# Waiting for each gather's landing by itself, with at most four gathers in flight, in a graph kernel's edge stage

## The chip, the cores and the metric

The kernel is one program on one core of a Trainium2 chip. The metric is the device time of one execution in microseconds (us), as the median of several runs.

## The reference

A layer on 3125 nodes of 256 features and 50,000 edges, sorted by destination. It adds to x a graph attention layer (8 heads, softmax over each destination's edges), a linear attention layer, and then a mixture of 16 experts, two for each node. What the change touches is the first:

```
def _L0_gnn_ref(x, edge_index, W, att_src, att_dst, ...):
    h = jnp.einsum('nf,hfd->hnd', x, W)
    a_s = jnp.einsum('hnd,hd->hn', h, att_src)
    a_d = jnp.einsum('hnd,hd->hn', h, att_dst)
    e = jax.nn.leaky_relu(a_s[:, src] + a_d[:, dst], 0.2)
    def head_step(acc, xs):
        h_h, e_h, g_h = xs
        m = jax.ops.segment_max(e_h, dst, num_segments=N)
        ex = jnp.exp(e_h - m[dst])
        den = jax.ops.segment_sum(ex, dst, num_segments=N)
        alpha = ex / den[dst]
        out = jax.ops.segment_sum(h_h[src] * alpha[:, None], dst, num_segments=N)
        return (acc + g_h * out, None)
...
xn = _layernorm(x, axis=-1)
x = x + gnn(xn, edges) + mix(xn)
x = x + ffn(_layernorm(x, axis=-1))
```

## The kernel before

Stages follow one another: projections and tables for the edges (up to about 190 us), the edge stage (190 to 1000 us), the output of both attentions, the experts, and the last sum. The edge stage holds the change.

The sum over edges is done on the features before W is applied, weighted for 8 heads. The 50,000 edges lie in 391 chunks (`CHUNKS`) of 128 edges. Destinations lie in 196 windows of 16 nodes. A step is a pair (chunk, window) that share an edge: the two lists are merged, so there are 391 + 196 - 1 = 586 steps, padded to 592, in 37 groups of `G` = 16. A chunk whose edges span two windows serves in two steps. Early windows have many edges, late ones few, so early groups take more new chunks than late ones.

For each chunk GpSimd gathers 128 rows of `node_rows` (272 floats each: 256 normalised features, a one, 8 source scores, padding; 128 x 1088 B = 136 KiB) into one slot of the ring `rows`, which has `RING` = 48 slots. The indices are a column of `srcT`. Nothing else runs on GpSimd in this stage, apart from five gathers of `gad` (64 KB each) at its start.

Readers of a slot are ScalarE's `copy_as` (L830, copies the source scores of 16 chunks to `asb`) and TensorE's `product` (L947, a matmul of `pw` with the chunk's row block into one of five PSUM banks `pO`). The order of a turn of the group loop is written out by hand for each engine in `groups([...])`. With tau as the turn, `copy_as` works at group tau, the scores, the running maxima and the exponentials at group tau - 1, the products, VectorE's `accumulate` (L790) and SyncE's stores of `agg_rows` (L986, two of 1 MB a group, 8 steps each) at group tau - 2. `accumulate` is a recurrence: each step's `acc` is the step's before, times `rsc` (L757 and L761, from TensorE's L922), plus the product.

Before `copy_as` of a group reads, ScalarE loads 16 slot numbers and the number of chunks needed into registers, then waits:

```
upto_chunk = act.value_load(step_tab[0:1, g, G:G + 1], min_val=1, max_val=CHUNKS)
act.wait_ge(fetched, upto_chunk)
```

GpSimd's queue before works in fours of gathers (`FETCH` = 4, 98 fours, the last of three). For a four that overwrites old slots, it loads a step number from `free_at` into a register (L679) and waits until so many products are done (`prod`, L680, a gate, with an increment of `s_gate` behind it at L681). The value belongs to the last of the four chunks being overwritten. It then issues four gathers that all raise the same one of two semaphores `s_rows`, and after that waits until the four before have landed and adds four to `fetched` (`landed`, the wait and the increment being one instruction, L675). At the time of that wait up to eight gathers may be under way.

The start of the stage also needs loads that SyncE issues: `adsd`, the bias `bg`, `WoT`, `bob`. VectorE waits for the last of them before its first work.

Of the kernel before, what the change touches and what calls it, by code (L numbers as in the profile page):

```python
# [29 lines left out]
CHUNKS = -(-NE // P)  # L30
# [3 lines left out]
G, HG = 16, 8  # L34
GROUPS = -(-STEPS // G)
# [5 lines left out]
RING, FETCH = 48, 4  # L41
FETCHES = -(-CHUNKS // FETCH)
# [84 lines left out]
def at_row(ap):  # L127
    return bass.IndirectOffsetOnAxis(ap=ap, axis=0)
# [32 lines left out]
def build(nc, a, out):  # L161

    with ExitStack() as top:
        def dram(name, shape, dt=F32):
            return nc.dram_tensor(name, shape, dt, kind="Internal").ap()

        def sb(name, shape, dt=F32, ctx=top):
            return ctx.enter_context(nc.sbuf_tensor(name, shape, dt))
# [4 lines left out]
        def sem(name):  # L173
            return top.enter_context(nc.semaphore(name))

        node_rows = dram("node_rows", (NP, RW))
# [44 lines left out]
        srcT = sb("srcT", [P, CHUNKS], U32, edge_ctx)  # L221
        step_tab = sb("step_tab", [1, SP_ // G, TAB], I32, edge_ctx)
        free_at = sb("free_at", [1, FETCHES], I32, edge_ctx)
# [365 lines left out]
        with ExitStack() as ctx:  # L589
# [5 lines left out]
            rows = sb("rows", [P, RING, RW], ctx=ctx)  # L595
# [39 lines left out]
            betaR = sb("betaR", [P, KD, P], ctx=ctx)  # L635
            v_cw, cw_ps = sem("v_cw"), sem("cw_ps")
            consts.expect(5)
            s_rows = [sem(f"s_rows{c}") for c in range(2)]
            s_flg, s_top = [sem(f"s_flg{c}") for c in range(V2)], sem("s_top")
            s_agg = [sem(f"s_agg{c}") for c in range(V3)]  # L640
            fetched, as_in = sem("fetched"), Count(sem("as_in"))
# [24 lines left out]
            with nc.Block() as block:  # L666
                @block.gpsimd
                def _(pool):

                    for j in range(SJ):  # L670
                        pool.indirect_dma_start(gad[:, j, :], None, ad_rows.rearrange("(w d) h -> w (d h)", d=DW), at_row(rowc[:, 1, j:j + 1])).then_inc(s_gad, 16)

                    def landed(q):
                        pool.wait_ge(s_rows[q % len(s_rows)], 16 * FETCH * (q // len(s_rows)) + 16 * len(range(q * FETCH, min((q + 1) * FETCH, CHUNKS))))
                        pool.sem_inc(fetched, len(range(q * FETCH, min((q + 1) * FETCH, CHUNKS))))  # L675

                    for q in range(FETCHES):
                        if q * FETCH >= RING:
                            steps = pool.value_load(free_at[0:1, q:q + 1], min_val=1, max_val=GROUPS * G)  # L679
                            pool.wait_ge(prod.sem, steps)  # L680
                            pool.sem_inc(s_gate, 1)  # L681
                        for k in range(q * FETCH, min((q + 1) * FETCH, CHUNKS)):
                            pool.indirect_dma_start(rows[:, k % RING, :], None, node_rows[:, :], at_row(srcT[:, k:k + 1])).then_inc(s_rows[q % len(s_rows)], 16)  # L683
                        if q:
                            landed(q - 1)
                    landed(FETCHES - 1)

                @block.vector
                def _(dve):
# [1203 lines left out]
```

## Time and profile before

| | us |
|---|---|
| median of 3 runs (lowest, highest) | 1812.19 (1808.88, 1820.98) |
| the profiled execution | 1812.91 |
| its span on the core | 1810.8 |
| TensorE busy in the span (matmul) | 1220.3 (67%) |
| VectorE | 1053.7 (58%) |
| ScalarE | 486.0 (27%) |
| GpSimd | 673.9 (37%) |
| mean DMA rate | 138 GB/s |

The span is the time from the first to the last instruction that the profile has. Busy time leaves out register, branch and semaphore instructions, so that a share says how long an engine computed, and not how near it is to being the limit. The ends of matmuls are modelled.

### The profile page before, as it was taken

What the parts mean: (1) busy time and instruction counts of PE and PEld (TensorE: products, weight loads), DVE (VectorE), ACT (ScalarE), POOL (GpSimd) and SP (SyncE); (2) the same over time, 40 slices, a digit from 0 to 9 for tenths busy, and PEclk for the clock granted to TensorE, in tenths of its full rate; (3) what the DMA queues carried; (4) which work ended last, traced back from release to release, by engine and by line L of the source; (5) the groups of instructions that cost most, each with busy time, mean ns of one, the idle gap of its engine ahead of it and who ended that gap; (6) DMA issues with size and microseconds to landing.
All of it is one profiled execution on the core that took longest, in us unless ns stands there. A gap on an engine that the chain in (4) does not pass through costs nothing. (4 is left out here: it accounts for less than half of the span.)

```text
span 1810.8 us, 29517 instructions
## 1 busy us (share of the span) xinstructions
PE 1220.3 (67%) x6148; PEld 994.7 (55%) x6149; DVE 1053.7 (58%) x3010; ACT 486.0 (27%) x1900; POOL 673.9 (37%) x781
## 2 busy tenths in 40 slices
PE   0795035666666776777784474999999179999800
PEld 0574023444444555555553353899998168999700
DVE  7656124556555666677785455678887433444357
ACT  0342011112221222222220233555553023333200
POOL 3000655656555454454300354244443201111164
PEclk9998556778887788897896656899999589999955
DMA  6015535566565656666644422334331395222155
GB/s 206 19 37 80 139 84 176 176 187 191 180 203 176 195 176 197 193 201 190 196 148 117 129 64 76 123 126 145 130 130 65 117 312 188 70 70 72 56 145 147
DMA packets 216712, 254.97 MB, mean 141 GB/s; under 512 B 53540, under 2 KB 190374, under 8 KB 212902
## 3 DMA queue, kind: packets, MB, share of 16 engines
q1 hardware_dynamic: 174262, 137.89, 24.9%
q0 software_dynamic: 30848, 103.40, 19.1%
q10 hardware_dynamic: 11504, 12.59, 2.1%
q8 instruction: 35, 0.57, 0.1%
q14 instruction: 63, 0.52, 0.1%
HBM read 138.88 MB, written 111.65 MB: 138 GB/s over the span
## 5 line engine op out<-in xcount | busy, mean ns | idle before, releaser
L683 POOL DMA_INDIRECT rows<-node_rows,srcT x391 | 381.7, 976 | 313.1 <-PE pO L947 179.7
L947 PE MATMUL pO<-rows,pw 128*128 x1184 | 381.1, 457 | 120.5 <-DVE pw L774 87.7
L790 DVE SCALAR_TENSOR_TENSOR acc<-acc,rsc,pO 128x257 f32<-128x257 f32 x592 | 282.4, 477 | 160.2 <-PE pO L947 74.0
L947 PEld LDWEIGHTS pO<-rows,pw 128*128 128x128 f32 x1184 | 243.0, 225 | 177.9 <-issue 143.2
L1355 PE MATMUL pW_<-W_again,aT 128*128 128x256 f32 x800 | 181.8, 381 | 0.0
L1355 PEld LDWEIGHTS pW_<-W_again,aT 128*128 128x128 f32 x800 | 148.9, 191 | 18.4
L1689 PEld LDWEIGHTS pHe<-xeT,w1e 128*128 128x128 f32 x1056 | 129.7, 194 | 9.9 <-DVE w1e L1727 6.6
L1689 PE MATMUL pHe<-xeT,w1e 128*128 128x128 f32 x1056 | 130.5, 277 | 5.7 <-DVE xeT L1707 4.8
L1745 POOL DMA_DIRECT2D ys_rows<-ye x66 | 35.7, 541 | 244.5 <-DVE ye L1737 244.5
L1698 PE MATMUL pYe<-w,hT 128*128 x528 | 125.3, 380 | 1.9 <-ACT hT L1668 1.1
L1668 ACT ACTIVATE hT<-pHe,b 128x128 f32<-128x128 f32 x264 | 75.5, 368 | 184.2 <-PE pHe L1689 172.7
L1698 PEld LDWEIGHTS pYe<-w,hT 128*128 128x128 f32 x528 | 95.2, 190 | 13.2 <-issue 3.0
L1406 DVE SCALAR_TENSOR_TENSOR own<-AG,al,own 128x256 f32<-128x256 f32 x200 | 94.8, 489 | 11.1 <-DMA AG<-agg_rows,lr 9.7
L830 ACT ACTIVATE asb<-rows 128x8 f32 x592 | 74.5, 209 | 70.0 <-issue 68.0
L774 DVE TENSOR_TENSOR pw<-pexp,eq 128x1024 f32<-128x1024 f32 x74 | 87.3, 1221 | 0.0
L1287 POOL DMA_INDIRECT xs_rows<-ysc,slot_x x50 | 49.4, 987 | 100.6 <-DVE slot_x L1510 91.7
L928 PE MATMUL pS<-topl,eq 128*128 128x72 f32 x148 | 29.4, 331 | 81.8 <-DVE topl L766 43.5
L1299 ACT ACTIVATE own<-xna,al 128x256 f32 (+1 forms) x200 | 82.2, 500 | 3.2 <-PEq L1039 2.5
L928 PEld LDWEIGHTS pS<-topl,eq 128*128 128x128 f32 x148 | 23.5, 227 | 96.2 <-DVE topl L766 53.9
L1727 DVE COPY w1e<-w 128x1024 f32 x66 | 45.8, 694 | 52.4 <-issue 39.0
L1707 DVE COPY xeT<-pXe 128x256 f32<-128x256 f32 x66 | 28.0, 424 | 79.6 <-PE pXe L1679 79.6
L1344 PE MATMUL pa<-cst,own 128*128 128x128 f32 x400 | 52.0, 286 | 18.6 <-DVE own L1406 18.6
(319 smaller groups left out, 2015.4 us busy)
## 6 DMA issues: line engine op xcount, KB each, us to landing
agg_rows<-acc SPq DMA_DIRECT2D x74, 1024.0 KB
w<-in_ffn_w SPq DMA_DIRECT2D x32, 512.0 KB, 5.6
xe<-xs_rows ACTq DMA_DIRECT2D x66, 128.0 KB, 2.0
ys_rows<-ye POOLq DMA_DIRECT2D x66, 128.0 KB, 2.0
rows<-node_rows,srcT POOLq DMA_INDIRECT x391
node_rows<-xna SPq DMA_DIRECT2D x25, 136.0 KB
xna<-in_x SPq DMA_DIRECT2D x5, 640.0 KB, 11.3
qs<-qT_y SPq DMA_DIRECT2D x25, 128.0 KB, 2.2
```

The costliest lines, as they stand in the source:

```text
L683: pool.indirect_dma_start(rows[:, k % RING, :], None, node_rows[:, :], at_row(srcT[:, k:k + 1])).then_inc(s_rows[q % len(s_rows)], 16)
L774: dve.tensor_tensor(pw[:, i, :, :].rearrange("p s (d h) -> p s d h", h=H), pexp[:, g % V2, s, :].unsqueeze(2).to_broadcast([P, HG, DW, H]) ...
L790: dve.scalar_tensor_tensor(out=acc[:, k % V3, s % HG, 0:D + 1], in0=before, scalar=rsc[:, g % V2, s:s + 1], in1=pO[n % PB][:, 0:D + 1], op ...
L830: ins = act.activation(asb[:, g % V2, s, :], rows[:, ds(at[s], 1), AS:AS + H].rearrange("p c h -> p (c h)"), ACT.Copy)
L928: mm = pe.matmul(td_ps[:, i * MW:(i + 1) * MW], eq[:, g % V3, i * HG:(i + 1) * HG, :].rearrange("p s d -> p (s d)"), topl[:, g % V2, i * H ...
L947: pe.matmul(pO[n % PB][:, 0:D + 1], pw[:, s // HG, s % HG, :], rows[:, ds(at[s % 4], 1), 0:D + 1].rearrange("p c f -> p (c f)"), start=Tru ...
L1299: ins = act.activation(own[:, c, h, :], tile(xna, t, 0, D), ACT.Copy, scale=al[:, 1, t, h:h + 1] if isinstance(t, int) else al[:, 1, ds(t, ...
L1355: mm = pe.matmul(pW[:, 0:D], aT[:, c, n, :], W[:, n % KD, n // KD, :], start=(n == 0), stop=(n == H * KD - 1))
L1406: ins = dve.scalar_tensor_tensor(out=own[:, c, h, :], in0=AG[:, c, h, :], scalar=al[:, 0, t, h:h + 1] if isinstance(t, int) else al[:, 0, ...
L1668: ins = act.activation(hT[:, c % 2, f, :], pH[c % 2][:, f * P:(f + 1) * P], ACT.Relu, bias=b1[:, ds(e, 1), f:f + 1].rearrange("p e f -> p ...
L1689: mm = pe.matmul(pH[c % 2][:, f * P:(f + 1) * P], w1e[:, c % S3, k, f * P:(f + 1) * P], xeT[:, c % 2, k, :], start=(k == 0), stop=(k == KD ...
L1698: mm = pe.matmul(pY[c % 2][:, 0:D], hT[:, c % 2, f, :], of_expert(w2, e, f), start=(f == 0), stop=(f == FK - 1))
```

## The change

GpSimd's queue goes gather by gather. There are four semaphores `s_rows`, and gather k raises number k mod 4. Before gather k is issued, gather k - 4 must have landed; that wait is one instruction with an increment of `fetched` by one. The gate is asked where it was asked before, at every fourth gather, behind that wait. The last four landings are waited for at the end. Ring, gate values, order of the gathers and all readers stay.

```diff
-            s_rows = [sem(f"s_rows{c}") for c in range(2)]
+            s_rows = [sem(f"s_rows{c}") for c in range(4)]
...
-                    def landed(q):
-                        pool.wait_ge(s_rows[q % len(s_rows)], 16 * FETCH * (q // len(s_rows)) + 16 * len(range(q * FETCH, min((q + 1) * FETCH, CHUNKS))))
-                        pool.sem_inc(fetched, len(range(q * FETCH, min((q + 1) * FETCH, CHUNKS))))
-
-                    for q in range(FETCHES):
-                        if q * FETCH >= RING:
-                            steps = pool.value_load(free_at[0:1, q:q + 1], min_val=1, max_val=GROUPS * G)
+                    def landed(k):
+                        pool.wait_ge(s_rows[k % len(s_rows)], 16 * (k // len(s_rows) + 1))
+                        pool.sem_inc(fetched, 1)
+
+                    for k in range(CHUNKS):
+                        if k >= len(s_rows):
+                            landed(k - len(s_rows))
+                        if k >= RING and k % FETCH == 0:
+                            steps = pool.value_load(free_at[0:1, k // FETCH:k // FETCH + 1], min_val=1, max_val=GROUPS * G)
                             pool.wait_ge(prod.sem, steps)
                             pool.sem_inc(s_gate, 1)
-                        for k in range(q * FETCH, min((q + 1) * FETCH, CHUNKS)):
-                            pool.indirect_dma_start(rows[:, k % RING, :], None, node_rows[:, :], at_row(srcT[:, k:k + 1])).then_inc(s_rows[q % len(s_rows)], 16)
-                        if q:
-                            landed(q - 1)
-                    landed(FETCHES - 1)
+                        pool.indirect_dma_start(rows[:, k % RING, :], None, node_rows[:, :], at_row(srcT[:, k:k + 1])).then_inc(s_rows[k % len(s_rows)], 16)
+                    for k in range(CHUNKS - len(s_rows), CHUNKS):
+                        landed(k)
```

## Rows read from the trace of the kernel before

A row of a timeline is: start us, duration us, engine, line, operation, names, count, and in brackets the idle time before it and its releaser. "issue" is idle time in which the engine waited for nothing that the profile shows; "remote" is a releaser that the profile matched to no instruction.

**Rows 1.** Groups of instructions by line, 192 to 970 us.
```profile
L683 POOL DMA_INDIRECT rows<-node_rows,srcT x391 | 381.7, 976 | 313.1 <-PE pO L947 179.7 <-issue 111.1 <-remote 21.8
L947 PE MATMUL pO<-rows,pw 128*128 x1180 | 380.3, 458 | 120.5 <-DVE pw L774 87.7 <-issue 31.5
L790 DVE SCALAR_TENSOR_TENSOR acc<-acc,rsc,pO 128x257 f32<-128x257 f32 x587 | 280.0, 477 | 159.7 <-PE pO L947 74.0 <-remote 38.7 <-issue 28.0
...
L830 ACT ACTIVATE asb<-rows 128x8 f32 x592 | 74.5, 209 | 70.0 <-issue 68.0 <-POOLq L675 1.6
```

**Rows 2.** Windows, accumulations of L790 alone: busy us (count), clock, DMA share, GB/s.
```profile
256.00:576.00 320.00, 108.62 (x228) 0.76 0.59 178
576.00:896.00 320.00, 133.11 (x280) 0.83 0.63 192
896.00:970.00 74.00, 38.23 (x81) 0.91 0.43 145
```

**Rows 3.** Windows, all engines (the count behind POOL is gathers).
```profile
256.00:576.00 320.00, 204.16 (x789) 149.17 (x790) 176.69 (x441) 64.18 (x384) 178.98 (x182) 0.76 0.59 178
576.00:896.00 320.00, 235.03 (x962) 172.66 (x963) 215.34 (x545) 75.84 (x446) 157.13 (x161) 0.83 0.63 192
```

**Rows 4.** Instructions of lines 675, 679, 681 on GpSimd's queue.
```profile
L675 POOLq EVENT_SEMAPHORE  x98: 17/17/17, 198.8 to 889.9; - x98
...
L679 POOLq TENSOR_LOAD <-free_at x86: 283/290/974, 249.2 to 876.6; - x86
L679 POOLq FUSED_REGOPS  x86: 147/147/186, 249.7 to 876.9; - x86
...
L681 POOLq EVENT_SEMAPHORE  x86: 17/17/17, 265.5 to 882.2; - x86
```

**Rows 5.** GpSimd's timeline, four of the gathers.
```profile
377.61 0.94 POOL L683 DMA_INDIRECT rows<-node_rows,srcT  x1 [5.07 <-issue]
...
405.86 0.95 POOL L683 DMA_INDIRECT rows<-node_rows,srcT  x1 [1.14 <-issue]
...
568.23 0.94 POOL L683 DMA_INDIRECT rows<-node_rows,srcT  x1 [2.62 <-issue]
...
783.01 0.94 POOL L683 DMA_INDIRECT rows<-node_rows,srcT  x1 [2.25 <-issue]
```

**Rows 6.** The tile rows, its gathers: duration ns, first and last start.
```profile
L683 POOL DMA_INDIRECT rows<-node_rows,srcT x391: 940/946/1961, 192.0 to 885.5; - x196
```

**Rows 7.** Timeline of all engines at two stretches.
```profile
233.01 0.45 PE L922 MATMUL pC<-shm,cst 128*128 128x16 f32 x2
...
243.37 0.28 ACT L858 ACTIVATE pexp<-pS 128x128 f32<-128x128 f32 x1 [11.25 <-remote]
...
251.32 0.95 POOL L683 DMA_INDIRECT rows<-node_rows,srcT  x1 [0.31 <-issue]
253.86 0.17 DVE L757 TENSOR_TENSOR rsc<-pC,firstT 128x16 f32<-128x16 f32 x1 [21.78 <-remote]
...
328.25 0.94 POOL L683 DMA_INDIRECT rows<-node_rows,srcT  x1 [0.30 <-issue]
...
331.56 0.48 DVE L790 SCALAR_TENSOR_TENSOR acc<-acc,rsc,pO 128x257 f32<-128x257 f32 x1 [7.76 <-remote]
```

**Rows 8.** The tile rsc: what ended VectorE's idle time before it (us, times).
```profile
  remote: 85.8, 21
```

**Rows 9.** Landings of the tiles gad, then agg_rows (its gathers).
```profile
DMA to landing us min/median/max: 2.4/2.6/2.8
...
DMA to landing us min/median/max: 5.5/5.8/7.9
```

**Rows 10.** Timeline at the stage's start.
```profile
212.83 0.56 DVE L697 TENSOR_SCALAR betaR<-cst,gam 128x128 f32<-128x128 f32 x2 [26.34 <-DMA bob<-in_bo]
...
221.81 1.37 ACT L830 ACTIVATE asb<-rows 128x8 f32 x11 [1.67 <-issue]
```

**Rows 11.** Window, all engines, 200 to 220 us.
```profile
200.00:220.00 20.00, 2.74 (x6) 1.47 (x6) 6.01 (x16) 0.24 (x1) 14.79 (x16) 0.50 0.85 208
```

## The prediction

> **What bounds the kernel now.** I began with the groups of instructions by line between 192 and 970 us, the edge stage, because the change touches nothing outside it [rows 1]. The reader is to see that no engine is full there: TensorE's products are 380 us of 778, VectorE's accumulation 280 us, and GpSimd's 391 gathers 382 us, with 313 us idle before them. 180 us of that idle time end with a TensorE product: it is the gate that frees slots of the ring.
>
> Then the windows [rows 2, 3]. Accumulations per window give the pace of the recurrence: 320/228 = 1.40 us a step from 256 to 576 us, 320/280 = 1.14 us from 576 to 896, and 74/81 = 0.91 us once the gathers are over (the last starts at 885.5 [rows 6]). GpSimd issued 182 and 161 gathers in the first two. At 0.91 us a step these 508 steps would take 464 us in place of 640. So 176 us of the stage go with the presence of gathers, though no engine shows that it waits for one.
>
> Where they go is seen in the timeline of all engines [rows 7]. TensorE's last matmul of the first group is recorded at 233.01 us; VectorE, which needs it, starts at 253.86 after 21.78 us idle, "remote", and ScalarE, which needs the one before, is late by 11.25 us. GpSimd issues 48 gathers in a row, the last at 251.32 for 0.95 us, so that VectorE goes on 1.6 us after it. At 331.56 the same: an accumulation has waited 7.76 us for a product recorded long before, and goes on 2.4 us after the run's last gather ended (328.25 + 0.94). I read this as TensorE's results being seen late while GpSimd issues back to back. There are 21 such waits of VectorE on this chain, 85.8 us in all [rows 8].
>
> **The change part by part.** *Signals.* The wait and the increment of `fetched` are one instruction of 17 ns on GpSimd's queue, 98 times before [rows 4]; there will be 391. The 293 more are 293 x 0.017 = 5.0 us of queue time, spread over a cadence of 1.25 us (0.95 busy, 0.30 issue) in which the queue already does 0.29 + 0.15 us of register work for every fourth gather [rows 4]. Cost 0; without that cover it would be 5 us.
>
> *When `fetched` rises.* Before, four arrivals are told at once, after the next four are issued; while the gate holds those back, the telling waits too. After, the first of four is told ahead of the gate and the other three behind it, each ahead of one more issue. So ScalarE hears earlier, by up to 5 us. Who waits for that? ScalarE's copies `asb` waited for this signal 1.6 us in all 37 groups, and 68.0 us for their own register loads ("issue") [rows 1]. TensorE reads the same chunks two groups later. Gain 0, at most 1.6 us.
>
> *The cap.* This is the wait that is added. Gather k now needs gather k-4 landed. Before, the first of a four needed the last of the four before the previous one, gather k-5, so a landing had 5 x 1.25 = 6.25 us, and now it has 4 x 1.25 = 5.00 us. Before, seven of the 97 boundaries between fours have a gap with releaser "issue" above the usual 0.30, the largest 1.14 us at 405.86 [rows 5]: landing plus reaction reached 6.25 + 0.84 = 7.1 us there, and stayed within 6.25 at the other 90. The trace gives these gathers no landing time. Nearest below are the gathers of `gad`, 64 KB each, 2.4 to 2.8 us; above, those of 1 MB from `agg_rows`, 5.5 to 7.9 us [rows 9]. One of these is 136 KB, nearer the small one. So most land well inside 5.0 us and are not delayed, and those beside a 1 MB store of `agg_rows` are. Each delay is between 0 and 7.1 - 5.0 = 2.1 us. On GpSimd that is at most 97 x 2.1 = 204 us of the 313 idle; I take 1 us beside each of the 64 stores of the groups that still have gathers, 64 us. Queued behind a blocked wait are only the next gathers and their signals, and for them ScalarE waits, once a group.
>
> What hides it is the ring's lead. ScalarE reads a group two groups ahead of the products. At 182/228 = 0.80 gathers a step, three groups of 16 steps hold 38 chunks of the ring's 48; 10 chunks, 12 steps x 1.40 = 17 us, are to spare. Later, at 161/280 = 0.58, it is 28 chunks, and 20 x 1.14 / 0.58 = 39 us are. A landing later by 2 us is not felt through `fetched`. Without the lead the 64 us would fall on the path.
>
> *Code.* Three gaps stand in the middle of a four, 5.07, 2.62 and 2.25 us, 112 gathers apart [rows 5]. I take them for GpSimd's instructions arriving late. The rows show 112 + 28 + 28 x 3 = 224 instructions for 112 gathers [rows 4]; after the change they are 112 + 112 + 28 x 3 = 308, so such a gap comes every 112 x 224/308 = 81 gathers: four in place of three, 2.3 to 5.1 us more of GpSimd's idle time, inside the 17 us. Cost 0.
>
> *The start.* VectorE waits 26.34 us for the load of `bob` until 212.83 [rows 10], while the gathers take their share of a DMA that is 0.85 busy at 208 GB/s [rows 11]. If the cap holds back up to three gathers of 139 kB there, the loads gain 0.42 MB / 208 GB/s = 2.0 us at most. I take 1. The 16 gathers that ScalarE needs at 221.81 are issued by 192.0 + 15 x 1.25 = 210.8; 11 us cover a slip.
>
> *Runs of gathers.* A gap for a landing lengthens a run. If results of TensorE come late until the run has ended, they come later by the gap: 21 waits x 0 to 2.1 us, 0 to 44 us. I take +2, near the lower end, since 90 of 97 boundaries kept within 6.25 us. That it frees something instead is the first rival.
>
> **The sum**: 1812.9 (the profiled execution; its span is 1810.8) - 1 + 2 = 1814. The median of the three runs is 0.7 lower than that execution, so 1813 us.
>
> **The rivals.** *Faster, because the cap eases TensorE.* What the 176 us go with is gathers in flight or back to back, and the cap thins them just where a store runs beside them. For it: the pace follows the number of gathers (182: 1.40, 161: 1.14, none: 0.91). Against it: the longest late result, 21.8 us, has an even cadence of 1.25 us beside no store, and if a landing takes 2.6 us there, two are in flight and the cap touches nothing. A quarter of 176 is 44 us, 1769; an eighth is 1791. It decides once a gap inside a run lets a pending result through.
>
> *Slower, because the runs end later.* 21 waits x 1 to 2.1 us = 21 to 44 us, 1834 to 1857. It decides from the point where landing plus reaction beside a store passes 5.0 us in nearly every group. For it: seven boundaries passed even 6.25. Against it: 90 did not.
>
> *The change does nothing*, because four are never in flight: 2.6/1.25 is two. Then 1812, within "same".
>
> *TensorE is not touched by gathers at all*, and the 176 us have another cause, such as fewer chunks a step. Then only the loads gain, 0 to 2 us: 1811 to 1813, within "same" too. The trace speaks against it, as late results and slow pace end with the gathers [rows 2, 7]; 0.1 of the 0.53 below is its. It is what the Trainium skill, "SBUF — State Buffer", section "SBUF: two separate sides", has: engine ports and DMA ports are disjoint, and TensorE waits for nobody there.
>
> **How the numbers follow.** My sum (the cap is hidden or never reached) 0.53, TensorE eased 0.24, runs lengthened 0.23. A measurement of this kernel tells about 1%, 18 us; its three runs spread by 12. The first case spans 1800 to 1828 and is all "same"; of each rival a little stays within 18 us. So faster by over 1% 0.23, within 0.55, slower 0.22. The range takes in about half of either rival: down to 1786 (a little over an eighth of the 176 us) and up to 1838 (21 waits x 1.2 us).
>
> **What would show it.** In the profile after: 391 signals of 17 ns; gathers 1.25 us apart but for gaps of 0.3 to 2 us inside the fours; idle time before the gathers near 313 us, less of it for `pO` and more for landings; `asb` still behind its register loads, with no wait for GpSimd's signal; the long mid-four gaps about 81 gathers apart; 1.40 and 1.14 us a step; the late result at 233 to 254 still there. I am wrong if the pace of steps moves by over 0.05 us (25 us in 508 steps), or if ScalarE waits for `fetched` in many groups.

## The result, and the profile after

| | before | after |
|---|---|---|
| median, us (lowest, highest, runs) | 1815.40 (1808.88, 1820.98, 4) | 1786.53 (1784.60, 1795.79, 4) |
| span of the profiled execution, us | 1810.8 | 1782.8 |

The ratio is 0.9854, with a 95% interval of 0.9823 to 0.9884: 1.5% faster. I had forecast 1813 us and no change.

The groups of instructions by line of the changed kernel, 192 to 970 us, which answer to [rows 1]:

```profile
L684 POOL DMA_INDIRECT rows<-node_rows,srcT x390 | 387.9, 995 | 284.5 <-PE pO L947 131.3 <-issue 110.0 <-DMA rows<-node_rows,srcT 35.7
L947 PE MATMUL pO<-rows,pw 128*128 x1184 | 380.2, 456 | 102.4 <-DVE pw L774 60.2 <-issue 40.3 <-DVE acc L790 0.5
L790 DVE SCALAR_TENSOR_TENSOR acc<-acc,rsc,pO 128x257 f32<-128x257 f32 x592 | 282.5, 477 | 159.3 <-remote 55.5 <-PE pO L947 55.4 <-issue 27.6
L830 ACT ACTIVATE asb<-rows 128x8 f32 x592 | 74.3, 209 | 67.9 <-issue 49.6 <-POOLq L675 18.0
```

The added wait is the third releaser of the first row: 35.7 us end with a landing. Its place was made by the gate, 179.7 us before and 131.3 now, and the whole idle time of GpSimd fell from 313.1 to 284.5 us. The last row names GpSimd's signal for 18.0 us of ScalarE's idle time, 1.6 before; that idle time as a whole is 67.9 us where it was 70.0, so nothing was added to it.

Windows of the changed kernel, accumulations alone, against [rows 2]:

```profile
256.00:576.00 320.00, 115.49 (x242) 0.77 0.63 190
576.00:896.00 320.00, 137.35 (x288) 0.86 0.63 193
896.00:970.00 74.00, 29.63 (x62) 0.84 0.47 132
```

That is 320/242 = 1.32 us a step where it was 1.40, and 320/288 = 1.11 where it was 1.14. TensorE's clock is not what changed the pace: it stood at 0.77 and 0.86 where it was 0.76 and 0.83, and a product took 456 ns on average where it took 458 [rows 1].

GpSimd's timeline of the changed kernel shows what a gap now looks like: four for a landing inside 30 us, then three that end with "issue":

```profile
273.97 0.95 POOL L684 DMA_INDIRECT rows<-node_rows,srcT  x1 [1.95 <-DMA rows<-node_rows,srcT]
281.93 0.94 POOL L684 DMA_INDIRECT rows<-node_rows,srcT  x1 [1.19 <-DMA rows<-node_rows,srcT]
290.72 0.95 POOL L684 DMA_INDIRECT rows<-node_rows,srcT  x1 [1.58 <-DMA rows<-node_rows,srcT]
302.51 0.95 POOL L684 DMA_INDIRECT rows<-node_rows,srcT  x1 [1.30 <-DMA rows<-node_rows,srcT]
366.49 0.95 POOL L684 DMA_INDIRECT rows<-node_rows,srcT  x1 [1.86 <-issue]
543.89 0.95 POOL L684 DMA_INDIRECT rows<-node_rows,srcT  x1 [1.56 <-issue]
756.73 0.95 POOL L684 DMA_INDIRECT rows<-node_rows,srcT  x1 [2.30 <-issue]
```

Gaps of 1.45 to 1.67 us with releaser "issue" stand at other places too, so that these three are taken for the three long gaps of [rows 5] only by their spacing.

Timeline of all engines at the first group, against [rows 7] and [rows 10]:

```profile
209.57 0.57 DVE L697 TENSOR_SCALAR betaR<-cst,gam 128x128 f32<-128x128 f32 x2 [25.17 <-DMA bob<-in_bo]
...
227.59 0.45 PE L922 MATMUL pC<-shm,cst 128*128 128x16 f32 x2
235.64 0.28 ACT L858 ACTIVATE pexp<-pS 128x128 f32<-128x128 f32 x1 [8.93 <-remote]
...
244.81 0.94 POOL L684 DMA_INDIRECT rows<-node_rows,srcT  x1 [0.30 <-issue]
245.45 0.17 DVE L757 TENSOR_TENSOR rsc<-pC,firstT 128x16 f32<-128x16 f32 x1 [18.78 <-remote]
...
246.06 1.93 POOL L684 DMA_INDIRECT rows<-node_rows,srcT  x1 [0.30 <-issue]
```

Here VectorE goes on in the middle of a run of gathers, with no gap of GpSimd beside it; in [rows 7] it went on behind the run's end.

Where the 28.0 us of span came from is read from first and last starts, before and after. The tile rows in the kernel before, its products:

```profile
L947 PE MATMUL pO<-rows,pw x1184: 377/380/797, 255.9 to 970.7; 128*128 x198
```

and in the changed kernel, products and gathers:

```profile
L947 PE MATMUL pO<-rows,pw x1184: 377/380/796, 247.5 to 945.7; 128*128 x198
L684 POOL DMA_INDIRECT rows<-node_rows,srcT x391: 943/949/1994, 189.9 to 862.4; - x196
```

The first product is 8.4 us earlier: 2.1 because the first gather is (192.0 before, 189.9 now), 3.3 more up to TensorE's L922 (233.01, 227.59), and 3.0 because its late result is less late (21.78, 18.78). That last part is no sign of the change: a second trace of the kernel before has 16.96 us there (e12 below). From the first product to the last it is 714.8 before and 698.2 after, 16.6 us less. The other 3.0 us lie behind the stage. So in this pair of traces more than half of the gain is pace in the middle of the stage.

### The profile page after: what moved, and what is told of

It reads as the page before. It is cut to its first block and busy times, and to the rows that moved or that the text cites. A ratio compares the mean times of both kernels' runs of the same rounds, so it can differ in the third digit from the quotient of the medians.

```text
span 1782.8 us, 29810 instructions
## 1 busy us (share of the span) xinstructions
PE 1216.7 (68%) x6148; PEld 991.9 (56%) x6149; DVE 1053.1 (59%) x3010; ACT 486.3 (27%) x1900; POOL 683.0 (38%) x781
## 3 DMA queue, kind: packets, MB, share of 16 engines
q1 hardware_dynamic: 174262, 137.89, 25.1%
## 5 line engine op out<-in xcount | busy, mean ns | idle before, releaser
L684 POOL DMA_INDIRECT rows<-node_rows,srcT x391 | 388.9, 995 | 284.9 <-PE pO L947 131.3
L790 DVE SCALAR_TENSOR_TENSOR acc<-acc,rsc,pO 128x257 f32<-128x257 f32 x592 | 282.5, 477 | 159.3 <-remote 55.5
L830 ACT ACTIVATE asb<-rows 128x8 f32 x592 | 74.3, 209 | 67.9 <-issue 49.6
```

The lines of the kernel that those rows point to most:

```text
L790: dve.scalar_tensor_tensor(out=acc[:, k % V3, s % HG, 0:D + 1], in0=before, scalar=rsc[:, g % V2, s:s + 1], in1=pO[n % PB][:, 0:D + 1], op ...
L830: ins = act.activation(asb[:, g % V2, s, :], rows[:, ds(at[s], 1), AS:AS + H].rearrange("p c h -> p (c h)"), ACT.Copy)
```

## The experiments

They were run in five groups, each group on one chip and beside its own runs of the kernel before. Their medians were 1806.0, 1810.6, 1804.0 and 1814.4 us in four groups (e1 to e4, e5 to e8, e12 to e15, e16 to e18), and 1647.6 us in the one of e9 to e11. Without this the ratios of e9 to e11 can't be understood; it became the main finding.

**e1: the signals without the cap.** The changed kernel with eight semaphores, so that gather k waits for gather k - 8. (Four of the semaphores are other, finished ones used again.)

```diff
-            s_rows = [sem(f"s_rows{c}") for c in range(4)]
+            s_rows = [sem(f"s_rows{c}") for c in range(8)]
...
```

> The changed kernel, with eight semaphores in place of four: each gather is waited for and told by itself, and up to eight may be in flight (four counters that older stages are done with are used again elsewhere, to have enough semaphores). Theory A (what helped is the cap of four, which thins the gathers beside the stores of agg_rows and lets TensorE's results come sooner): back to the time of before, ratio 0.995 to 1.005, 1.40 and 1.14 us a step. Theory B (what helped is that each landing is told as it comes): ratio 0.983 to 0.988 as with the change, 1.32 and 1.11 us a step.

Measured 1810.32 us, ratio 1.0025 [0.9988, 1.0062]. Telling of each gather is worth nothing by itself; what gained is the cap. ScalarE's wait for GpSimd's signal is here too (19.6 us in 12 waits), so the 18.0 us of the changed kernel do not come from its cap either.

**e2: the cap without the signals.** At most four in flight, but `fetched` raised by four.

```diff
-                        pool.sem_inc(fetched, 1)
+                        if (k + 1) % FETCH == 0 or k == CHUNKS - 1:
+                            pool.sem_inc(fetched, k % FETCH + 1)
```

> The changed kernel, but fetched rises by four once the fourth of a four has landed; the cap of four stays. Theory A (the cap): ratio 0.983 to 0.988 as with the change. Theory B (each landing told): ratio 0.995 to 1.005. If ScalarE's copies wait for the signal in many groups here, B gains.

Measured 1790.78 us, 0.9911 [0.9873, 0.9948]. Most of the gain is there with the cap alone. Whether telling singly adds the rest is not settled, since the interval overlaps that of the whole change. The late results before rsc are not fewer here: 91.9 us in 28 waits.

**e3 and e5: a cap of three and of two.**

```diff
-            s_rows = [sem(f"s_rows{c}") for c in range(4)]
+            s_rows = [sem(f"s_rows{c}") for c in range(3)]
```

> The changed kernel with three semaphores: at most three gathers in flight. Theory A (the cap): below the change's 1787 us, 1765 to 1785, since more gathers are held apart; GpSimd's idle time for landings rises from 36 to 100 us or more. Theory B (each landing told): 1785 to 1795, as with the change, or a little slower by the later landings. A third theory, C (the cap costs and something else gained): 1800 or more.

> The changed kernel with two semaphores: at most two gathers in flight. Theory A (fewer in flight ease TensorE): the results of TensorE come late for less than the 109 us of the kernel with three, but a gather that lands 2.5 us after its issue, plus 1.1 us of reaction, sets 1.8 us a gather in place of 1.25, 391 x 1.8 = 704 us for the whole, near the length of the stage; so the time is at 1760 to 1800 us, and ScalarE's copies wait for the signal. If the late results depend on the number of gathers alone: as late as with three, and 1790 or more.

e3: 1774.71 us, 0.9860 [0.9787, 0.9933]. e5: 1962.96 us, 1.0865 [1.0799, 1.0931]. The tile rsc in the kernel before had "remote: 85.8, 21" [rows 8]; in the changed kernel and then in e3:

```profile
  remote: 87.0, 24
```

```profile
  remote: 23.6, 10
```

In e5 there is no such line at all: with two in flight no wait of VectorE or ScalarE ends with "remote". But GpSimd then issues too slowly: its gathers come (1088.8 - 190.7) / 390 = 2.30 us apart, where I had expected 1.8 and a time of 1760 to 1800 us.

The 23.6 us of e3 are too low. Its first group has a late result as well, which the profile puts down to "issue": TensorE's L922 is recorded at 227.78 for 0.45 us, and then

```profile
247.12 0.18 DVE L757 TENSOR_TENSOR rsc<-pC,firstT 128x16 f32<-128x16 f32 x1 [20.26 <-issue]
```

With it e3 has 43.9 us. The two further traces with a cap of three where results were late (e8 and e18, with a hold described below) have 35.3 and 46.4. One trace tells this number only roughly: without a cap it is 70.5 to 99.1 us in four traces (e14, the kernel before, e12, e1), and with a cap of four 64.5, 87.0 and 91.9 (e13, the changed kernel, e2). Idle time by releaser in e3 and e5, tile rows: e3 first, then e5. "POOLq L675" is ScalarE waiting for a signal:

```profile
  DMA rows<-node_rows,srcT: 135.6, 84
  POOLq L675: 73.4, 25
```

```profile
  POOLq L675: 358.9, 36
  DMA rows<-node_rows,srcT: 327.8, 166
```

So a cap trades late results for late gathers: at three the late results are about half of what they are without a cap, at two there are none, and ScalarE's wait is 73 and 359 us. At four neither differs clearly from the kernel without a cap.

**e4 and e8: a hold that breaks the first run.** The first 48 gathers follow each other without a gate. Here the 33rd waits until the first group's weights are out; e4 is the kernel before with it, e8 has the cap of three too.

```diff
+                        if q * FETCH == 32:
+                            pool.wait_ge(pw_in.sem, 1)
+                            pool.sem_inc(s_gate, 1)
```

> The kernel before, with one wait more: GpSimd issues its first 32 gathers and then waits until VectorE has its first pw (the first group's weights), and only then the other 16 of the first run. If TensorE's results are late because gathers are issued back to back: the 20.4 us between TensorE's last matmul of group 0 (233 us) and VectorE's use of it falls to under 4 us, and the whole is 14 to 20 us faster than before (ratio 0.989 to 0.992). If the late results have another cause (code loading, the clock, the matmuls themselves): the 20 us stay, and the whole is equal or slower, ratio 1.000 to 1.010.

> At most three in flight, and the wait of e4 at the 33rd gather. In e4 the first product came 21 us earlier and all of it was given back, because the gathers (last one at 885 us in both) set the pace behind it. If the cap of three leaves the gathers less in the way, a part stays: 1755 to 1770. If the gathers are the pace here too: as with the cap of three alone, 1770 to 1780.

e4: 1795.19 us, 0.9960 [0.9924, 0.9996]; e8: 1770.23 us, 0.9791 [0.9734, 0.9848]. The tile rows in e4, products, and the timeline of e4 at the first group:

```profile
L950 PE MATMUL pO<-rows,pw x1184: 380/380/797, 234.5 to 970.4; 128*128 x198
```

```profile
232.47 0.17 DVE L760 TENSOR_TENSOR rsc<-pC,firstT 128x16 f32<-128x16 f32 x1 [5.25 <-remote]
```

The late result of the first group shrank as expected (5.25 us in place of 21.78), and the first product came 21.4 us earlier. GpSimd's last gather before the hold ends at 229.87 (228.92 + 0.95), and VectorE goes on 2.6 us later. In e8 and e18 it is the same: the last gather before the hold ends at 238.09 and 238.74, and VectorE goes on 3.3 and 3.5 us later, at 241.35 and 242.19. This is the plainest sign that a pause of GpSimd lets a pending result through. But the last product came only 0.3 us earlier, and the gain of 14 to 20 us that I expected was about 7. Most of the early start is given back in the middle: the windows have 225 and 276 steps where 228 and 280 were. How much is less sure, for the traced execution took 1807.24 us, 12 more than e4's median. In e8 the hold's share is not settled, since its interval overlaps that of e3.

**e6 and e7: bytes or descriptors.** The gathers behind the 48th fetch 64 bytes a row in place of 1088 (e6), or are plain copies of a whole tile of `node_rows` (e7). Both leave out the real gather behind the 48th and so sum over wrong features; they only tell times, each from one execution.

```diff
...
+                            else:
+                                pool.indirect_dma_start(rows[:, k % RING, 0:16], None, node_rows.rearrange("n (a b) -> (n a) b", b=16), at_row(srcT[:, k:k + 1])).then_inc(s_rows[q % len(s_rows)], 16)
```

```diff
...
+                            else:
+                                pool.dma_start(rows[:, k % RING, :], row(node_rows, k % NT)).then_inc(s_rows[q % len(s_rows)], 16)
```

> The kernel before, but all gathers behind the 48th fetch 64 B a row in place of 1088 B (the rest of each slot keeps what the first 48 brought): as many descriptors and as much work on GpSimd, a seventeenth of the bytes. If the bytes that the gathers move make TensorE's results late: behind the first group the late results are gone, a step takes 0.95 us or less, and the whole is 140 us or more faster (under 1680). If the writing of descriptors does it: 1790 to 1815, no change of pace.

> The kernel before, but behind the 48th gather each is replaced by a plain copy of 128 consecutive rows, from the same queue of GpSimd: the same bytes, no list of indices, 0.54 us of GpSimd each in place of 0.95 (the sums are over other rows). If the bytes make TensorE's results late: pace as before, 1.40 and 1.14 us a step, 1790 to 1815. If GpSimd's reading of indices and writing of descriptors does it: 1.0 to 1.1 us a step, 1700 to 1760.

e6: 1804.18 us beside 1810.58 (1794.13 to 1815.10). e7: 1656.84 us, less than the 1700 to 1760 expected. The same tile rsc in e6, then in e7:

```profile
  remote: 106.9, 28
```

```profile
  remote: 25.4, 2
```

The 25.4 us of e7 belong to the first 48 gathers, which are still indirect. The transfers after them, by line, e6 and e7:

```profile
L686 POOL DMA_INDIRECT rows<-node_rows,srcT x343 | 336.2, 980 | 291.1 <-PE pO L950 168.0 <-issue 94.7 <-remote 27.8
```

```profile
L686 POOL DMA_DIRECT2D rows<-node_rows x343 | 181.8, 537 | 301.1 <-PE pO L950 286.4 <-issue 14.5
```

A seventeenth of the bytes changes nothing beyond the scatter; the same bytes without indirect gathers take 154 us off. What holds the results back goes with GpSimd's indirect gathers, not with the data that they move. Of the gathers, e7 changes several things at once, the list of indices, the scattered rows and GpSimd's 0.95 us a transfer (0.54 for a copy), and does not say which of them it is. The Trainium skill, "SBUF — State Buffer", section "SBUF: two separate sides", has engine ports and DMA ports disjoint; e6 agrees with it as far as bytes go.

**e9 to e11: the group in which nothing was late.** e9 is the kernel before with register loads behind every four gathers, meant as a pause; e10 and e11 repeat e3 and e8.

```diff
+                        for _ in range(3):
+                            pool.value_load(free_at[0:1, 0:1], min_val=0, max_val=GROUPS * G)
```

> The kernel before, with three register loads behind every four gathers on GpSimd's queue. By the rows of its loads (0.29 us and 0.15 us of register work each) that is a pause of about 1.3 us after every 5 us, whatever has landed, with up to eight gathers in flight as before; 98 x 1.3 = 129 us, inside the 313 us that GpSimd idles before its gathers. Theory: what holds TensorE's results back is an unbroken run of gathers, and a gap lets them through. Then this does what the cap of three does: 1.1 to 1.3 us a step, ratio 0.975 to 0.99, fewer and shorter late results ('remote' before rsc well under 85.8 us). Rival: what counts is how many gathers are in flight, or what a landing does to GpSimd. Then the pace stays at 1.40 and 1.14 and the ratio at 0.995 to 1.005, or a little slower. A third: register loads on GpSimd's queue are no gap for whatever the results wait for; then the late results stay or grow, since runs take longer: 1.00 to 1.03.

> Cap of three again, with more rounds, beside the next run on the same chip: 0.986 before, 0.978 to 0.990 expected.

> Cap of three with the 33rd gather held until the first group's weights are out, again. It gave 0.979 where the cap alone gave 0.986, with overlapping intervals. If the hold adds its 5 to 10 us here it is 0.978 to 0.982 and below the run beside it; if the gain is given back later, as in the kernel before with the hold alone, the two are equal within 0.4%.

The kernel before took 1647.60 us (1640.68 to 1651.66, 17 runs). e9: 1653.45 us, 1.0035 [1.0017, 1.0053]. e10: 1738.49 us, 1.0557 [1.0531, 1.0584]. e11: 1746.09 us, 1.0577 [1.0549, 1.0606]. My expectations for all three were wrong: the version found best is 5.8% slower here. The tile rsc in e9, all the releasers above 1 us:

```profile
  PE pO L949: 35.9, 109
  PE pC L924: 19.8, 37
  issue: 11.7, 35
```

No "remote", with 391 gathers as dense as ever. Windows of e9, accumulations alone, then GpSimd's and ScalarE's rows in e10:

```profile
256.00:576.00 320.00, 142.81 (x300) 0.87 0.76 230
```

```profile
L684 POOL DMA_INDIRECT rows<-node_rows,srcT x391 | 391.1, 1000 | 297.1 <-DMA rows<-node_rows,srcT 170.1 <-issue 93.2 <-PE pO L947 33.8
L830 ACT ACTIVATE asb<-rows 128x8 f32 x592 | 72.8, 209 | 169.2 <-POOLq L675 162.4 <-issue 6.8
```

The pace in e9 is 320/300 = 1.07 us a step, so gathers are wanted faster, and with the cap of three ScalarE waits 162.4 us for them (50.7 in e9). With nothing late, a cap of three has only its cost. The hold brings nothing here either.

**e12 to e15: the same question with a trace of the kernel before.** e12 is the kernel before, e13 the changed one, e14 repeats e9 and e15 repeats e7.

> The kernel before, once, so that the session has a trace of it beside the next three. Theory A (two regimes of a session: in one TensorE's results come late while GpSimd issues indirect gathers back to back, in the other they do not): where its time is near 1810 us, 'remote' before rsc is near 85 us in 21 times; where it is near 1648 us, there is no 'remote' before rsc and the pace is under 1.1 us a step. Theory B (the 160 us come from a faster chip or clock as a whole): every stage is shorter, the projections before 190 us and the experts too, by about 9%.

> The changed kernel beside it. Theory A: near 1786 us and ratio 0.985 where the kernel before takes 1810; where that takes 1648, there is nothing that a gap could free and the waits for landings alone are left, so 1.00 to 1.04 (the cap of three gave 1.056). Theory B: 0.985 in either.

> Three register loads behind each four gathers, again. Where the kernel before takes 1648: 1.0035 again. Where it takes 1810: if a gap of any kind lets TensorE's results through, 0.975 to 0.99; if it must be a landing, or fewer in flight, 0.995 to 1.01.

> The kernel before with the gathers behind the 48th as plain copies of a tile of node_rows into the same slot, same bytes (so the features that are summed are others). It gave 1657 us where the kernel before took 1811. Theory A: 1650 to 1660 us in either regime, since without indirect gathers nothing is held back; so the same as the kernel before where that takes 1648. Theory B: 154 us less than the kernel before in either, so 1494 where that takes 1648.

The kernel before took 1803.98 us. e12: 1801.74. e13: 1782.00, 0.9878 [0.9844, 0.9913], the change's gain again, with 242 and 301 steps in the two windows where e12 has 233 and 279. (The traced execution of e13 took 1772.85 us, 9 less than its median.) e14: 1805.04, 0.9993 [0.9960, 1.0026]. e15: 1655.00. The tile rsc in e12, then in e13:

```profile
  remote: 95.8, 29
```

```profile
  remote: 64.5, 25
```

The late result of the first group in e12:

```profile
246.39 0.94 POOL L683 DMA_INDIRECT rows<-node_rows,srcT  x1 [0.31 <-issue]
247.19 0.17 DVE L757 TENSOR_TENSOR rsc<-pC,firstT 128x16 f32<-128x16 f32 x1 [16.96 <-remote]
247.64 0.95 POOL L683 DMA_INDIRECT rows<-node_rows,srcT  x1 [0.30 <-issue]
```

The same kernel as in [rows 7] has it 4.8 us shorter, and it ends inside the run of gathers, as in the changed kernel.

The 1648 us and the 1655 us of plain copies are nearly one number: taking the indirect gathers away gives about what the undisturbed group had with them. A whole chip that is quicker by 9% is excluded, for the stretch before the edge stage took the same (first gather at 191.1 us in e9, 192.7 in e12). TensorE's clock is a rival for a part only. From 190 us to the end of the last product, with the same instructions, e12 and then e9 (the first number behind the comma is TensorE's busy time, the third from the end its clock):

```profile
190.00:968.10 778.10, 513.71 (x2039) 376.50 (x2039) 463.09 (x1158) 161.39 (x961) 383.71 (x393) 0.77 0.59 178
190.00:834.20 644.20, 474.70 (x2039) 345.77 (x2039) 461.94 (x1158) 160.89 (x961) 387.42 (x392) 0.86 0.71 215
```

The stretch is 133.9 us shorter, of 144.8 us between the two spans, and TensorE's busy time 39.0 us. The higher clock can have given at most these 39.

e14 did not do what I had meant. GpSimd's timeline in e14, the first and last gather of a four and the first of the next:

```profile
399.16 0.94 POOL L683 DMA_INDIRECT rows<-node_rows,srcT  x1 [7.66 <-PE pO L949]
...
402.91 0.95 POOL L683 DMA_INDIRECT rows<-node_rows,srcT  x1 [0.30 <-issue]
404.16 0.95 POOL L683 DMA_INDIRECT rows<-node_rows,srcT  x1 [0.30 <-issue]
```

Three register loads stand between 402.91 and 404.16, and no gap is seen. They are worked off while GpSimd is busy with the gathers. As a test of gaps e9 and e14 say nothing. By chance e14 has one gap of 4.06 us at the first group, from 232.65 to 236.71, and there VectorE takes TensorE's result of 235.35 after 1.79 us.

**e16 to e18: real gaps without a cap.** GpSimd waits for all landings behind every eighth gather (e16; every sixteenth in e17).

```diff
-                        if q:
+                        if q % 2:
                             landed(q - 1)
-                    landed(FETCHES - 1)
+                        if q % 2 == 1:
+                            landed(q)
```

> The kernel before, but behind every eighth gather GpSimd waits until all have landed: a true gap of about 2.5 us (a landing, by the row of gad) plus reaction, after every 10 us, with up to eight gathers in flight in between. Theory 1 (an unbroken run of gathers holds TensorE's results, any real gap of GpSimd frees them): the late results are cut to under 10 us each, 'remote' before rsc is half of 90 us or less, and the time is 1 to 3% under a kernel before of about 1805, unless GpSimd's own pace, (8 x 1.25 + 3.3) / 8 = 1.66 us a gather, becomes the limit: 391 x 1.66 = 650 us, under the 695 it takes now. Theory 2 (what counts is the number in flight): as the kernel before, or slower. Where the kernel before takes 1648: 1.03 to 1.06, as the cap of three.

> The same behind every sixteenth gather: a gap after every 20 us. Theory 1: a third to a half of what e16 gains, since most runs between gates are shorter than 16 gathers anyway. Theory 2: as the kernel before.

> Cap of three with the hold once more: 0.975 to 0.985 if the kernel before takes about 1805 beside it, 1.05 to 1.06 if it takes 1648.

e16: 1812.10 us, 0.9990 [0.9961, 1.0019]. e17: 1821.42 us, 1.0033 [1.0002, 1.0064]. e18: 1779.01 us, 0.9814 [0.9778, 0.9851]. The timeline of e16 at the first group:

```profile
228.39 0.45 PE L923 MATMUL pC<-shm,cst 128*128 128x16 f32 x2
228.88 0.17 DVE L758 TENSOR_TENSOR rsc<-pC,firstT 128x16 f32<-128x16 f32 x1 [1.41 <-issue]
...
231.50 1.05 POOL L683 DMA_INDIRECT rows<-node_rows,srcT  x1 [2.60 <-DMA rows<-node_rows,srcT]
...
422.71 0.94 POOL L683 DMA_INDIRECT rows<-node_rows,srcT  x1 [3.24 <-issue]
...
435.75 1.51 POOL L683 DMA_INDIRECT rows<-node_rows,srcT  x1 [3.32 <-issue]
```

TensorE's matmul ends at 228.84, just as a gap of GpSimd begins, and VectorE goes on at 228.88: the first group has no late result. Late results as a whole are down as well, and ScalarE's wait for GpSimd is up:

```profile
  remote: 53.9, 24
```

```profile
L831 ACT ACTIVATE asb<-rows 128x8 f32 x592 | 75.2, 209 | 104.6 <-issue 61.6 <-POOLq L675 42.9
```

So half of theory 1 stands, that gaps make late results fewer, and its price fails: 53.9 us, less than any trace without a cap or with a cap of four has, bring nothing. A round of eight takes 435.75 - 422.71 = 13.0 us, 1.63 us a gather; at 0.80 gathers a step that is 1.30 us a step, about the pace that was to be won (the changed kernel has 1.32). That GpSimd's own pace ate the gain is argued, and not the whole of it: e16 has 221 steps in the window from 256 to 576 us, 1.45 us a step, and GpSimd still waited 81.1 us for the gate. In e17 nothing came of the expected third or half of a gain: 83.3 us of late results, and a time that is the same or a little longer. e18 came as expected.

## Why the prediction was wrong

**The step that failed** is *Runs of gathers*, and with it the choice between my sum and the first rival. I took +2 us from 0 to 44, because a gap for a landing lengthens a run and the results of TensorE would come later by the gap; "that it frees something instead" had a chance of 0.24. The sign was the other one. The gain comes with the cap (e1, e2), and the pace moved from 1.40 to 1.32 us a step, past the 0.05 us that I had set for myself; the second pair of traces, e12 and e13, has 1.37 and 1.32, and in the later window 1.15 and 1.06 (1.14 and 1.11 in the first pair). The rival priced it at 44 us (a quarter of the 176) or 22 (an eighth); 28 were measured, about a sixth.

Behind the +2 stood a reading of [rows 7] that did not hold: that a late result goes on only once the run has ended. There it went on 1.6 us behind the run's end. In the changed kernel and in e12 it goes on inside the run, with gathers 1.25 us apart on both sides of it. So a longer run need not mean a later result.

My argument against the rival, that an even cadence leaves two in flight and the cap never bites, was wrong as well: the cap was reached in 32 gaps, 35.7 us (22 gaps and 25.1 us in e13). Whether these gaps let results through is not shown. They are 35.7/32 = 1.1 us long on average, where VectorE went on 2.6 to 3.5 us into the pauses of e4, e8 and e18, and the longer but fewer gaps of e16 gain nothing.

How far the mechanism is shown: the cap is the cause of the gain (e1, e2; e13 repeats the gain); late results go down clearly at a cap of three and wholly at two (e3, e5); they go with indirect gathers, not bytes (e6, e7); and with no late results the cap of three only costs (e10). At a cap of four the profile does not separate it. "Remote" before rsc is 87.0 against 85.8 us in one pair of traces, and 64.5 against 95.8 in the other. How a cap of four gains is therefore an inference from the caps of three and two.

*Signals*: right. 391 of 17 ns, and e1 bounds their cost at about 11 us, with 4.5 measured and zero inside its interval.

*When `fetched` rises*: I forecast no wait of ScalarE for the signal; it has 18.0 us in 11 waits. They cost nothing that can be seen, since its idle time before these copies is no longer than before. The gain taken, 0, stands within what e2 can tell.

*The cap*: GpSimd's delays were put at 64 us and are 35.7. That the ring's lead hides them holds at a cap of four: the gate's waits fell by 48.4 us, more than the delays. At three and two it does not.

*Code*: wrong, without effect. Three gaps still stand about 110 gathers apart, and not four with 81 between them; single signals did not count as I had counted them. That such gaps are instructions arriving late was my reading, and no run shows it.

*The start*: right. VectorE's wait for `bob` ends 3.3 us earlier, of which 2.1 belong to an earlier start of the stage; 1.2 are left of the 0 to 2 that I gave.

*TensorE is not touched by gathers at all* fell with e5 and e7. *Slower, because the runs end later* did not happen at four; e5 shows the same waits deciding at a cap of two.

The range, down to 1786, just held the time, because it took in an eighth of the 176 us. That was luck at its edge: the sum behind the 1813 had the sign of the cap's effect wrong.

**What stays open**: what differs between the group that took 1648 us and the four that took 1804 to 1814. It is not the chip alone, for the group of e1 to e4 and that of e9 to e11 carry the same chip number. It stayed the same through the 17 runs of the kernel before in its group. What the changed kernel with its cap of four does there was not tried; the cap of three costs 5.6%. Nor is it settled how the cap of four gains, and why many short gaps gain where fewer long ones do not. And of GpSimd's indirect gathers it is open what holds the results back.

## What to carry to other kernels

A result that is recorded done and seen late, and goes on when another engine pauses, is a cost of its own: test it by changing that other engine's work (fewer in flight, another kind of transfer), not its bytes. A cap on transfers in flight has an optimum with two prices, here late results of about 44 and 0 us against late gathers of 73 and 359 us at caps of three and two; read both before choosing it. Count late results in more than one trace, and look at long waits of any name: the kernel before gave 85.8 and 95.8 us, the same with register loads that did nothing 70.5, and one wait of 20.26 us stood under "issue". Time a version in more than one group of runs, beside the kernel before each time: the cap of three, in two of them with the hold, was 0.979 to 0.986 in three groups, and 1.056 in a fourth.

## What the runs showed of the hardware

- The same kernel took 1640.68 to 1651.66 us in one group of 17 runs and 1791.13 to 1832.05 in the others, with no difference before the edge stage (first gather at 191.1 and 192.7 us). In the slower groups TensorE's results are seen up to 21.78 us late while GpSimd issues indirect gathers of 0.95 us back to back; in the three traces of the quick group no wait of VectorE or ScalarE in the edge stage ends with "remote". 133.9 of the 144.8 us between e12 and e9 lie in or ahead of the edge stage's last product, at most 39 of them by the granted clock (0.77 and 0.86).
- Where the run of gathers was broken, a late result was seen 2.6, 3.3 and 3.5 us later (e4, e8, e18); where it was not, it was seen within the run, 15.6 us (e12) and 17.4 us (the changed kernel) behind its matmul's recorded end.
- An indirect gather keeps GpSimd for 0.95 us whether a row has 64 or 1088 bytes; a plain copy of the same 136 KB keeps it for 0.54 us, and no result was late beside those (e7, e15).
- Three register loads of 0.29 us each on GpSimd's queue behind a gather made no gap before the next one, 0.30 us as elsewhere (e14).
- An earlier start can be given back: the first product came 21.4 us earlier in e4, and the last 0.3.
